# Layer 2 attention: the rows of p are scaled by one over their sum before they are turned, by GpSimd and ScalarE, in place of a scaling of the mixed result

## The reference

```python
q = split_heads(inputs @ Wq)
k = split_heads(inputs @ Wk)
v = split_heads(inputs @ Wv)
scores = jnp.einsum('bnqd,bnkd->bnqk', q, k) + position_bias
attn = jax.nn.softmax(scores, axis=-1)
hidden = jnp.einsum('bnqk,bnkd->bnqd', attn, v)
return hidden @ Wo
```

## Time and profile before

| | |
|---|---|
| runs | 2488.57, 2495.5, 2509.12 us; median 2495.5 |
| profiled execution | 2481.91 us |
| its span | 2480.2 us |
| TensorE busy | 2074.4 us, 84% of the span |
| VectorE busy | 1439.5 us, 58% |
| ScalarE busy | 1188.4 us, 48% |
| GpSimd busy | 468.6 us, 19% |
| the stage | about 751 to 1745 us of the span |

### The profile page before, as it was taken

One profiled execution on the slowest core, in us unless ns is written; L12 is line 12 of the kernel. 1 busy time (PEld: TensorE's weight loads), 2 busy tenths in 40 slices (PEclk: granted clock), 3 DMA queues, 4 the chain that ended last, 5 costly groups with the idle time before them and its releaser, 6 DMA issues. The chain is left out here.

```text
span 2480.2 us, 41334 instructions
## 1 busy us (share of the span) xinstructions
PE 2074.4 (84%) x14039; PEld 1335.6 (54%) x14039; DVE 1439.5 (58%) x4030; ACT 1188.4 (48%) x2412; POOL 468.6 (19%) x546
## 2 busy tenths in 40 slices
PE   3435998468679999999999999999793589999888
PEld 3224995437555555555555555555693244444447
DVE  4675223542266777777776777776465566666415
ACT  1122553234336666666666666666133125555543
POOL 0164551153511111111100000000264200000000
PEclk9866998668869999999999999999897557888869
DMA  3413662046450000000000000001474232232001
GB/s 127 129 42 99 229 227 77 1 143 208 139 145 22 10 10 10 10 10 10 10 3 1 1 1 1 1 9 44 136 257 142 72 109 64 64 96 90 6 1 35
DMA packets 120233, 173.06 MB, mean 70 GB/s; under 512 B 16136, under 2 KB 79344, under 8 KB 119584
## 3 DMA queue, kind: packets, MB, share of 16 engines
q1 hardware_dynamic: 108016, 141.38, 18.1%
q0 software_dynamic: 11584, 23.91, 2.8%
q10 hardware_dynamic: 432, 5.19, 0.5%
HBM read 68.27 MB, written 45.40 MB: 46 GB/s over the span
## 5 line engine op out<-in xcount | busy, mean ns | idle before, releaser
L1808 ACT ACTIVATE t_p<-t_p,t_low 128x512 f32<-128x512 f32 x512 | 369.4, 722 | 333.6 <-DVE t_low L1879 333.5
L1879 DVE CUSTOM_DVE_ANT_0 t_p<-bank,L_skewed 128x512 f32<-128x512 f32 x512 | 332.6, 687 | 276.8 <-PE bank L1701 276.8
L129 PE MATMUL pair<-ident,t_p 128*128 128x128 f32 x2048 | 279.9, 280 | 0.0
L129 PEld LDWEIGHTS pair<-ident,t_p 128*128 128x128 f32 x2048 | 219.0, 141 | 94.8 <-issue 92.5
L2216 ACT ACTIVATE alibi_p<-pair 128x1024 f32<-128x1024 f32 (+1 forms) x192 | 168.8, 883 | 193.8 <-PE pair L2103 193.5
L2275 DVE CUSTOM_DVE_ANT_0 alibi_junk<-bank,alibi_later 128x512 bf16<-128x512 f32 (+1 forms) x256 | 150.8, 623 | 106.2 <-PE bank L2115 103.6
L1958 POOL COPY t_wide<-t_inverse 128x512 f32<-128x512 f32 x64 | 39.1, 611 | 893.0 <-DVE t_inverse L1895 884.2
L2115 PE MATMUL bank<-alibi_k_aug,alibi_q_aug 32*128 32x512 f32 (+1 forms) x256 | 107.7, 584 | 36.0 <-DMA alibi_k_aug<-aug_k 16.4
L1701 PEld LDWEIGHTS bank<-t_k_hi,t_q_hi 64*128 64x128 f32 x512 | 47.7, 183 | 161.5 <-issue 149.6
L1701 PE MATMUL bank<-t_k_hi,t_q_hi 64*128 64x512 f32 x512 | 127.8, 496 | 3.5 <-DVE t_low L1879 3.2
L1723 PE MATMUL pair<-t_pT,t_v 128*64 128x512 f32 x512 | 123.8, 605 | 1.5 <-DVE t_hT L1902 1.5
(11 more groups left out here) (488 smaller groups left out, 4450.0 us busy)
## 6 DMA issues: line engine op xcount, KB each, us to landing
L0moe_w<-L_packed SPq DMA_DIRECT2D x39, 578.0 KB, 3.4
L2moe_w<-L_skewed SPq DMA_DIRECT2D x39, 450.0 KB, 3.1
L1moe_w<-L_packed SPq DMA_DIRECT2D x23, 578.0 KB, 3.4
alibi_q_aug<-aug_q SPq DMA_DIRECT2D x8, 1024.0 KB, 7.7
alibi_k_aug<-aug_k SPq DMA_DIRECT2D x8, 1024.0 KB, 7.8
L_skewed<-bias_table SPq DMA_DIRECT2D x16, 448.0 KB, 9.5
slots<-g ACTq DMA_DIRECT2D x3, 1690.0 KB, 10.4
L0moe_xs<-slots SPq DMA_DIRECT2D x39, 130.0 KB, 3.2
```

The source lines that it names most:

```text
L129: last = nc.tensor.transpose(out[0:piece.shape[1], j * P:j * P + piece.shape[0]], piece, ident[0:piece.shape[0], 0:piece.shape[0]])
L1808: nc.scalar.activation(p[:, u % RING, :], p[:, u % RING, :], ACT.Exp, bias=low[:, u % 16:u % 16 + 1], scale=-1.0, accum_out=sums[:, n % 2, ...
L1879: nc.vector.tensor_tensor_reduce(out=p[:, u % RING, :], in0=score_ps[h][:], in1=skewed[:, (n % PAIRS) * 2 + h, start:start + SEQ], scale=- ...
```

## The change

The rows of p are multiplied by one over their sum while still in SBUF, before the transposes. For each unit that is one 128x512 instruction with a per-row factor: six units of a step on GpSimd (both halves of tiles 0 and 2, half 0 of tiles 1 and 3), two on ScalarE (`divide`, half 1 of tiles 1 and 3). The reciprocal becomes four instructions of 128x2 a step (`invert(n, t)`). `wide`, `turn_scale`, `store_scale` and `scale` are gone, and `norm` is a plain copy of the mixed bank, on ScalarE instead of VectorE. The ring of p has six units, the scores run two tiles ahead of the transposes, and `k_product` runs two steps ahead.

```diff
-    PAIRS, HALF, RING = HEADS // 2, P // 2, 4
+    PAIRS, HALF, RING = HEADS // 2, P // 2, 6
...
-            return (n, t + 1) if t + 1 < TPS else (n + 1, 0)
+            return (n, t + 2) if t + 2 < TPS else (n + 1, t + 2 - TPS)
...
             def turns(n, t):
                 for h in range(2):
                     u = unit(n, t, h)
-                    pe.wait_ge(expd, u + 1)
+                    if t % 2 and h:
+                        pe.wait_ge(act_divided, by_act(n, t) + 1)
+                    else:
+                        pe.wait_ge(divided, by_pool(n, t, h) + 1)
...
             for n in range(STEPS + 2):
-                live = n < STEPS
-                if live:
-                    scores(n, 1)
-                    turns(n, 0)
-                if n + 1 < STEPS:
-                    q_product(n + 1)
-                    k_product(n + 1)
+                live, more = n < STEPS, n + 1 < STEPS
                 if live:
                     scores(n, 2)
+                    turns(n, 0)
+                if more:
+                    q_product(n + 1)
+                if live:
+                    scores(n, 3)
                     turns(n, 1)
                 if 1 <= n <= STEPS:
                     mix(n - 1, 0)
                 if live:
-                    scores(n, 3)
                     turns(n, 2)
+                if 1 <= n <= STEPS:
+                    mix(n - 1, 1)
...
-                if 1 <= n <= STEPS:
-                    mix(n - 1, 1)
-                if n + 1 < STEPS:
+                if more:
                     scores(n + 1, 0)
                 if live:
                     turns(n, 3)
                 if n >= 2:
                     output(n - 2)
-                if 1 <= n <= STEPS:
-                    turn_scale(n - 1)
-                if n + 1 < STEPS:
+                if more:
+                    scores(n + 1, 1)
                     v_product(n + 1)
+                if n + 2 < STEPS:
+                    k_product(n + 2)
...
+            def divide(n, t):
+                u = unit(n, t, 1)
+                act.wait_ge(inverted, n * TPS + t + 1)
+                nc.scalar.activation(p[:, u % RING, :], p[:, u % RING, :], ACT.Identity,
+                                     scale=inverse[:, n % 2, t * 2 + 1:t * 2 + 2]).then_inc(act_divided, 1)
+
+            def norm(n):
+                act.wait_ge(mixed, n + 1)
                 if n >= 1:
-                    act.wait_ge(normed, n)
-                nc.scalar.copy(scale[:], kc_ps[:]).then_inc(scaled, 1)
+                    act.wait_ge(added, n)
+                nc.scalar.copy(hT[:], mix_ps[:]).then_inc(normed, 1)
...
                     if n < STEPS:
                         m, s = after(n, t)
+                        if t >= 2:
+                            move(n, t)
                         if m < STEPS:
                             exponents(m, s, 0)
-                        move(n, t)
+                        if t % 2 == 0:
+                            divide(n, t + 1)
+                        if t < 2:
+                            move(n, t)
                         if m < STEPS:
                             exponents(m, s, 1)
+                    if t == 0 and n >= 2:
+                        norm(n - 2)
...
+                for t in range(TPS):
+                    for h in range(2 - t % 2):
+                        u = unit(n, t, h)
+                        pool.wait_ge(inverted, n * TPS + t + 1)
+                        nc.gpsimd.tensor_scalar(p[:, u % RING, :], p[:, u % RING, :], inverse[:, n % 2, t * 2 + h:t * 2 + h + 1],
+                                                None, ALU.mult).then_inc(divided, 1)
```

More of the change, by code:

```diff
@@ L1637, in t5_attention_block @@
         low, sums, inverse = st.sb("low", [P, 16]), st.sb("sums", [P, 2, 8]), st.sb("inverse", [P, 2, 8])
-        wide, scale = st.sb("wide", [P, 8, HALF]), st.sb("scale", [P, SEQ])
         hT, sT = st.sb("hT", [P, SEQ]), st.sb("sT", [P, SEQ])
@@ L1645, in t5_attention_block @@
         moved = [st.sem("moved0"), st.sem("moved1")]
-        mixed, inverted, widened = st.sem("mixed"), st.sem("inverted"), st.sem("widened")
-        scale_made, scaled, normed = st.sem("scale_made"), st.sem("scaled"), st.sem("normed")
+        mixed, inverted, normed = st.sem("mixed"), st.sem("inverted"), st.sem("normed")
+        divided, act_divided = st.sem("divided"), st.sem("act_divided")
         sent = st.sem("sent")
@@ L1656, in unit, with by_pool, by_act @@
             return n * 8 + t * 2 + h
+        def by_pool(n, t, h):
+            return n * 6 + (t // 2) * 3 + (t % 2) * 2 + h
+        def by_act(n, t):
+            return n * 2 + t // 2
         def after(n, t):
-            return (n, t + 1) if t + 1 < TPS else (n + 1, 0)
+            return (n, t + 2) if t + 2 < TPS else (n + 1, t + 2 - TPS)
         @block.tensor
@@ L1671, in k_product @@
             def k_product(n):
-                if n >= 3:
-                    pe.wait_ge(scaled, n - 2)
-                elif n >= 1:
+                if n >= 1:
                     pe.wait_ge(k_low, n)
@@ L1726, in mix @@
                     ins.then_inc(mixed, 1)
[L1728 to L1732, removed]
             def output(n):
@@ L1752, in _ @@
             scores(0, 0)
+            k_product(1)
+            scores(0, 1)
             for n in range(STEPS + 2):
-                live = n < STEPS
-                if live:
-                    scores(n, 1)
-                    turns(n, 0)
-                if n + 1 < STEPS:
-                    q_product(n + 1)
-                    k_product(n + 1)
+                live, more = n < STEPS, n + 1 < STEPS
                 if live:
                     scores(n, 2)
+                    turns(n, 0)
[3 more added lines that the diff above has]
+                    scores(n, 3)
                     turns(n, 1)
@@ L1827, in _ @@
             store_v(0)
-            exponents(0, 0, 0)
-            exponents(0, 0, 1)
-            for n in range(STEPS + 1):
+            for t in range(2):
+                exponents(0, t, 0)
+                exponents(0, t, 1)
+            for n in range(STEPS + 2):
                 for t in range(TPS):
@@ L1889, in move, with invert @@
                                       turn_ps[0][:].rearrange("p (j n) -> p j n", n=P)).then_inc(moved[0], 1)
-            def invert(n):
-                dve.wait_ge(expd, (n + 1) * 8)
+            def invert(n, t):
+                dve.wait_ge(expd, unit(n, t, 1) + 1)
                 if n >= 2:
[L1894 to L1902, removed]
+                    dve.wait_ge(divided, by_pool(n - 1, 0, 0))
+                    dve.wait_ge(act_divided, by_act(n - 1, 0))
+                nc.vector.reciprocal(inverse[:, n % 2, 2 * t:2 * t + 2], sums[:, n % 2, 2 * t:2 * t + 2]).then_inc(inverted, 1)
             def sum_out(b):
@@ L1918, in _ @@
             low_k(0)
-            bias(0, 0, 0)
-            bias(0, 0, 1)
-            for n in range(STEPS + 2):
-                for t in range(TPS):
[L1923 to L1927, removed]
-                        move(n, t)
-                    if t == 0 and 1 <= n <= STEPS:
-                        invert(n - 1)
+            for t in range(2):
+                bias(0, t, 0)
+                bias(0, t, 1)
+            invert(0, 0)
+            for n in range(STEPS):
+                for t in range(TPS):
+                    m, s = after(n, t)
+                    if t + 1 < TPS:
+                        invert(n, t + 1)
+                    elif n + 1 < STEPS:
+                        invert(n + 1, 0)
+                    if t >= 2:
+                        move(n, t)
+                    if m < STEPS:
+                        bias(m, s, 0)
+                        bias(m, s, 1)
+                    if t < 2:
+                        move(n, t)
                     if t == 0 and n + 1 < STEPS:
+                        cut_k(n + 1)
+                        low_k(n + 1)
+                    if t == 1 and n + 1 < STEPS:
                         cut_q(n + 1)
                         low_q(n + 1)
[L1934 to L1938, removed]
                     if t == 1 and n % PAIRS == 2 and PAIRS <= n < STEPS:
```

13 lines of the change are left out of this document (3 added, 10 removed).

## The result

| | before | after |
|---|---|---|
| median of four executions | 2492.45 us | 2663.31 us (2657.2 to 2671.74) |
| ratio | | 1.0665 [1.0614, 1.0715] |
| profiled execution, its span | 2481.91, 2480.2 us | 2666.98, 2665.2 us |
| stage, first exponent to last | 756.68 to 1730.85: 974.2 us | 766.43 to 1899.87: 1133.4 us |

The change makes the kernel 6.7% slower: 171 us, where 107 were forecast. The stage holds 159.3 us of it, 2.5 a step.

A forecast was written before the change was run, and what follows sets the result against it. The prediction took TensorE's own row as the bound; -0.32 (work) + 1.85 (tile 3) + 0.17 (`norm`) = +1.70 us a step, times 63 = +107 us, on 2492.0 gave 2599 us, range 2560 to 2668.

The forecast's parts named there:

- The bound and the sign: In the changed stage TensorE's row is the bound, every wait lengthens the step fully; slower was given 0.95.
- The wait at tile 3: TensorE's half 1 transposes wait for ScalarE's divide, behind the next step's tile 0 exponents: 1.85 us a step.
- the step that failed: GpSimd's 128x512 multiplication taken as 1.0 us, between a copy's 0.61 and a two-input subtraction's 1.27, adding no wait.
- The rule beside it: At tile 2, each 0.1 us of GpSimd's multiplication above 1.27 adds 2 x 0.1 x 63 = 13 us.
- the rival that carried it: GpSimd's multiplication is slower than any row in the trace, delaying tile 2; 2641 us at T = 1.6, chance 0.07.
- a sign that it was wrong: In the new profile, GpSimd's multiplication over 1.27 us and releasing TensorE would show the forecast wrong.
- `norm`: right place, too short: The first piece of mix waits for the norm copy on ScalarE: 0.17 us a step, between 0 and 0.4.
- TensorE's work: Without the scale's four transposes a step's work falls from 15.32 to 15.00 us: -0.32 a step, 20 us in all.
- the two bounds: TensorE's work of a step after the change: 15.07 us at most, 14.89 at least.
- The clock: Forecast 1.00 in the stage; rival: falls of 1.7 us after the new wait, every second step 2653 us, chance 0.17.
- The sum: Over 63 steps of the stage, -0.32 + 1.85 + 0.17 = +1.70 us a step, +107 us.
- the cases called slower: Forecast as summed 0.65, falling clock 0.17, slower GpSimd 0.07, shorter tile 3 wait 0.07; together stated as 0.95.

The follow-up runs named there:

- the run with two inputs: Changed kernel with GpSimd multiplying p by the factor spread over the row as a second input (tensor_tensor) instead of tensor_scalar: 2625.11 us, ratio 1.0532.
- four and four: Changed kernel with half 0 of every tile multiplied by GpSimd, half 1 by ScalarE, each divide heading the turn of the tile before: 2476.91 us, ratio 0.9926.

## Why the prediction was right in kind and short in size

*The bound and the sign: right.* TensorE's row was the bound, and every wait in it came through in full: three waits, taken away one by one, took the step from 17.75 to 15.87, 15.34 and 15.07.

*The wait at tile 3: right.* 1.85 forecast, 1.84 measured. Bias 0.10 after half 0 (0.11 forecast), exponent 0.83 (0.84), divide 1.55 (1.56), TensorE on at 2.31 (2.32). The divide takes 0.707 us; the exponent, same shape with one operand per row, was the right row to read it from.

*GpSimd: the step that failed.* "I take 1.0, nothing in the sum hanging on it between these ends." The ends, 0.61 and 1.27, were both passed: 1.565. I had taken it that one wide input lies between a copy and a subtraction of two. The runs show that a factor per row costs GpSimd more (1.565 us) than a second wide input does (1.271, and 1.039 with the repeated factor). The rule beside it held: from 1.27 on, twice the excess on tile 2. That makes 2 x 0.295 = 0.59 a step; 0.51 came, because the `mix` in front was itself 0.1 later than in the sum. This one term is 32 to 35 of the 64 us missing, and the rival that carried it (2641 at T = 1.6) had a chance of 0.07 only. With no row of the operation itself that was too low. The prediction had also named this as a sign that it was wrong, a multiplication over 1.27 us that releases TensorE, and by that sign it was.

The Trainium skill, "GPSIMD Engine Reference", section "4.1 Engine selection", has GpSimd about two times slower than VectorE for two inputs and roughly at line rate for one. The copy of one input agrees with that order (0.611 us against 1.271 for two); the multiplication does not, if a factor per row counts as one input: 1.565 us, against 1.039 for the form with two. No run here has the same product on VectorE.

*`norm`: right place, too short.* 0.17 forecast, 0.27 measured. The copy ended at 3.92 behind tile 0's start, as summed (1417.39), but `mix` started 0.15 later and not 0.04: a handover read between VectorE and ScalarE was put on TensorE. Between the divide and TensorE it is 0.05. 6 us in all.

*TensorE's work: slightly too good.* -0.32 taken, -0.25 measured (15.07), the upper of the two bounds: the neighbours that might have given up to 0.18 back gave nothing. 4 us.

*The clock: right as a mechanism, rare here.* The forecast said 1.00 in the stage. The clock did fall after the new wait, as the rival had it, but in 2 of the 63 steps of the kernel after and in 4 of those of the run with two inputs; in the six other runs of the changed kernel, where the wait at tile 3 is gone, the stretch from 800 us to the stage's end is at 1.00. A fall cost 1.6 us, where 1.7 were forecast, so the price was right; 32 falls had been taken, and 2 came. Why it falls in these steps and not in the others, no run shows. The Trainium skill, "TensorE: Matmul & The Clock Gate", "A second HAM failure mode: psum-queue depth-cycling", has a clock that swings under frequent short idle times. Here an idle 1.66 us in every step did not do that: the steps between the falls stayed at 1.00.

*The sum.* (-0.25 + 1.87 + 0.54 + 0.27) x 63 = 153 where 107 stood. The stage shows 159, the medians 171. Of the 64 us, 46 are these terms, 6 the rest of the stage with the two falls of the clock, and 12 are outside the stage, where executions of one kernel differ by as much.

*The range: luck in part.* 2663 lies in 2560 to 2668, but the upper end was there for falls of the clock in every second step (2653), which did not come. The sum with GpSimd at T = 1.6 was 2641. What filled the range up was another term than the one that it had been stretched for. The chances carry a slip too: the cases called slower add up to 0.96, not 0.95.

## What to carry to other kernels

When an engine's order is written by hand and that engine is the bound, go through each new operation and ask what stands in front of it on its own engine, and what that in turn waits for: one divide behind one exponent cost 120 us, while all eight multiplications of a step cost nothing once none of them was late (four and four). Where an operation is in no row of the trace, don't bound it by rows that look alike on both sides; put the point from which it decides beside it, and give the far side a real chance. A slow form need not be replaced where its length can be hidden: four and four, with the slow form still in it, is as fast as the kernel without any multiplication. Six and two comes within 3.3 us of that kernel's stage once the shorter form is used and two calls are moved. And look at which term fills a range in the end: here it was not the one that the range had been stretched for.

## What the runs showed of the hardware

- GpSimd, 128x512 in f32: a factor per row as a scalar operand 1.565 us, the same product with the factor as a repeated second input 1.039 us. A copy was 0.611 and a subtraction of two real inputs 1.271. Why the form with a scalar operand is slowest was not tried.
- ScalarE's product with a factor per row was 0.71 to 0.73 us, less than half of GpSimd's.
- From the end of ScalarE's copy to the `mix` that waits for it 0.15 us pass; from the divide to the transposes 0.05.
- With an idle 1.66 us in front of tile 3's second transposes in every step, the granted clock went to the lower level in 2 of 63 steps (four times in the run with two inputs), each time right after that wait, for 1.6 us of loss each time in the kernel after.
